# Layer 1 as eight pairs of tiles: the two tiles between the layers join the pair scheme, and the weight sums are split into parts while layer 0 still runs

## The reference

```
y0 = einsum('bct,bcd->bdt', x, W0[cond])           # layer 0, mix
x  = x + y0 @ (sign(w) * (|w| >= 0.05) * mean|w| by column) + b0
y1 = einsum('bct,bcd->bdt', x, W1[cond])           # layer 1, mix
w1 = NF4_LEVELS[q_weight] * q_scale (by groups of 64), out x in
x  = x + y1 @ w1.T + bias + 4 * (y1 @ A.T) @ B.T
```

## Time and profile before

| | |
|---|---|
| median of 3 runs | 357.35 us (357.08 to 357.49) |
| the profiled execution | 358.29 us, its span 356.5 us |
| PE busy | 348.7 us, 98% of the span |
| DVE, POOL, ACT busy | 232.8, 233.2, 165.5 us |
| chain that ended last | PE 92% |
| DMA | 44.63 MB, mean 125 GB/s |

### The profile page before, as it was taken

The page is one execution under the profiler, slowest core; times in us unless marked ns, Lnnn a source line. Parts: engine busy times, 40 slices in busy tenths (PEclk is TensorE's granted clock), DMA queues, the critical chain, the costliest instruction groups (busy, mean ns, idle before and its releaser), DMA issues.

```text
span 356.5 us, 5523 instructions
## 1 busy us (share of the span) xinstructions
PE 348.7 (98%) x1820; PEld 295.6 (83%) x1820; DVE 232.8 (65%) x354; ACT 165.5 (46%) x298; POOL 233.2 (65%) x153
## 2 busy tenths in 40 slices
PE   6899999999999999999999999999999999999996
PEld 6668788888888888888888888888888888888884
DVE  5689968999999999995859336155362552624523
ACT  2688367878887887772535305013040130411300
POOL 0388999998877987778511666567365673666632
PEclk9999999999999999999999999999999999999999
DMA  6894411753454345324421301505115042150202
GB/s 242 270 340 142 155 31 30 270 205 126 138 165 156 118 153 187 146 71 173 142 103 63 120 0 65 180 0 187 58 64 182 0 162 83 62 181 2 118 29 90
DMA packets 27838, 44.63 MB, mean 125 GB/s; under 512 B 8834, under 2 KB 17026, under 8 KB 27810
## 3 DMA queue, kind: packets, MB, share of 16 engines
q1 hardware_dynamic: 26242, 43.67, 35.3%
q10 hardware_dynamic: 1568, 0.61, 0.6%
HBM read 27.49 MB, written 16.78 MB: 124 GB/s over the span
## 4 chain that ended last, share of the span: by engine, by line
PE 92%; POOL 2%; SPq 1%; DMA 1%; ACT 1%; DVE 1%; issue 1%; POOLq 0%; ACTq 0%
PE acc L1208 37%; PE acc L1170 31%; PE xT L1134 11%; PE acc L1150 6%; PE spare L1134 4%; POOL col_scale L617 2%; PE acc L1236 2%; DMA w_in<-in_L_ffn_w 1%; PE acc L1238 1%; PE xT L1217 1%; SPq L447 0%; SPq L445 0%; SPq L466 0%; ACT w_in L718 0%; PE xT L1225 0%
## 5 line engine op out<-in xcount | busy, mean ns | idle before, releaser
L1170 PE MATMUL acc<-T,hh 128*128 128x512 f32 x192 | 76.0, 396 | 0.0
L1170 PE MATMUL acc<-T,hl 128*128 128x512 f32 x192 | 75.1, 391 | 0.0
L590 POOL TENSOR_TENSOR X<-X,bias 128x1024 f32<-128x1024 f32 x28 | 67.2, 2401 | 11.3 <-PE xT L1134 9.7
L1208 PE MATMUL acc<-W,hh 128*128 128x512 f32 x224 | 71.3, 389 | 0.0
L744 ACT ACTIVATE spare<-q_raw 128x512 f32<-128x512 int32 x96 | 56.0, 599 | 18.6 <-DVE side_p L944 6.3
L1032 DVE TENSOR_TENSOR X<-X,acc 128x512 f32<-128x512 f32 x42 | 28.8, 687 | 40.5 <-PE acc L1208 21.4
L649 POOL TENSOR_TENSOR X<-X,ys 128x512 f32<-128x512 f32 x21 | 26.4, 1286 | 36.6 <-DVE ys L1021 36.6
L1208 PEld LDWEIGHTS acc<-W,hh 128*128 128x128 f32 x224 | 42.1, 188 | 8.7
L1208 PE MATMUL acc<-W,hl 128*128 128x512 f32 x112 | 43.6, 389 | 0.0
L1170 PEld LDWEIGHTS acc<-T,hl 128*128 128x128 f32 x192 | 36.1, 188 | 7.4
L1134 PEld LDWEIGHTS xT<-mix,X 128*128 128x128 f32 x336 | 40.8, 192 | 1.4
(11 more groups left out here) (99 smaller groups left out, 652.1 us busy)
## 6 DMA issues: line engine op xcount, KB each, us to landing
out<-X SPq DMA_DIRECT2D x26, 512.0 KB, 2.9
X<-out SPq DMA_DIRECT2D x16, 512.0 KB, 3.5
X<-in_x SPq DMA_DIRECT2D x12, 512.0 KB, 3.4
q_raw<-in_L_ffn_q_weight SPq DMA_DIRECT2D x16, 256.0 KB, 2.9
w_in<-in_L_ffn_w SPq DMA_DIRECT2D x14, 256.0 KB, 6.6
x_first<-in_x SPq DMA_DIRECT2D x4, 512.0 KB, 4.2
out<-x_first SPq DMA_DIRECT2D x4, 512.0 KB, 4.7
out<-X SPq DMA_DIRECT2D x4, 256.0 KB, 2.0
```

The costliest lines, as they stand in the source:

```text
L590: pool.tensor_tensor(x_of(g), x_of(g), bias[:, :], ALU.add).then_inc(s_xb, 1)
L1170: mm = pe.matmul(acc[:, bank_of(q), :], a[:, k, :], b, start=(k == 0 and j == 0), stop=(k == KB - 1 and j == len(terms) - 1))
L1208: mm = pe.matmul(acc[:, bank, :], a[:, k, :], w1(part, c, k), start=(k == 0 and j == 0), stop=(k == HB - 1 and j == len(terms) - 1))
```

## The change

Layer 1 begins with the first pair at once: tiles 16 and 17 are pair 0 of eight (`SB` = 16). The direct multiplication, its residual add and its store are gone. B12, which only the direct tiles used, gets no high and low part; the sums are formed from the whole copy of it. The transposes of the pieces with d % 4 other than 1 come one slot earlier, so that no slot behind 30 has one.

The parts of the sums move. `SPLIT` now lists T1, T2 and T3 for the first three blocks, then their last blocks, then T4. In slot 29 (the second half of tile 14) ACT and DVE make parts 0 to 3, in slot 30 parts 4 to 8, in slot 31 part 9, behind it 10 and 11, and the four of T4 one ahead of each of the first takes of pair 0 (`LATE`), since they lie where layer 0's weight was. In slot 31 ACT also does the copy of A21 and the high part of S1, ahead of part 9; DVE does S1 to S4 ahead of it. The result of tile 15 goes into POOL's list between the low parts of S1 and S2. The first two products change places (A11 x B11, then A12 x B21), and with them the copy of the product that ACT makes. Bank 2 is free for product 2 when tile 15's second half has left it (`s_ys`), bank 3 when all sums are made. On SP tile 15's spill, then the load of tile 19, come ahead of the first pair's store.

```diff
-    SB = NT + 2
-    NP = (2 * NT - SB) // 2
+    SB = NT
+    NP = NT // 2
...
-    PRODUCTS = ((A12, B21, 0), (A11, B11, 1), (S1, T1, 2), (S2, T2, 3), (S3, T3, 0), (S4, B22, 1),
+    PRODUCTS = ((A11, B11, 0), (A12, B21, 1), (S1, T1, 2), (S2, T2, 3), (S3, T3, 0), (S4, B22, 1),
                 (A22, T4, 2))
...
-    W_ORDER = [(B11, 1), (B12, 1), (B21, 1), (B22, 1), (B11, 0), (B12, 0), (B21, 0), (B22, 0),
-               (T1, 0), (T1, 1), (T2, 0), (T2, 1), (T3, 0), (T3, 1)]
-
-
-    SPLIT = (T4, T1, T3, T2)
-    NTS = len(SPLIT)
-    SUMS_BY = (0, 4, 8, 12, NTS * HB)
+
+    W_ORDER = [(B11, 1), (B21, 1), (B22, 1), (T1, 1), (B11, 0), (B21, 0), (B22, 0), (T1, 0),
+               (T2, 0), (T2, 1), (T3, 0), (T3, 1)]
+    NW = len(W_ORDER) + 2
+
+
+    SPLIT = ([(c, j) for c in (T1, T2, T3) for j in range(HB - 1)] + [(c, HB - 1) for c in (T1, T2, T3)]
+             + [(T4, j) for j in range(HB)])
+    NTS = 4
+    SPLIT_BY = {NH * NT - 3: 0, NH * NT - 2: 4, NH * NT - 1: 9, NH * NT: 10}
+    LATE = (12, 13, 14, 15, 16)
...
-    def sums_by(m):
-
-        return SUMS_BY[m - NH * NT]
...
     def turned_in(d):
-
-        return max(NH * F, ready_in(d) + 2) + (d % 4 != 1)
+        return max(NH * F, ready_in(d) + 2)
+
+    def blocks_before(d):
+
+        return sum(BLOCK[e % 4] != B12 for e in range(d))
...
+        side_S1 = sb("side_S1", [P, 2, BANK], F32R)
+        plain_sums = sb("plain_sums", [P, KB - 2, BANK], F32)
         W_T4 = sb("W_T4", [P, 2, HB, BANK], F32R)
-        side_S1 = sb("side_S1", [P, 2, BANK], F32R)
-        plain_sums = sb("plain_sums", [P, NH * KB - 2 * HB - 2, BANK], F32)
...
-                at = w1(part, B12, {S4: 0, A22: 2}[o])
+                at = (W01 if o == S4 else W23)[:, NW - 2, part, :]
...
         def bank_free(eng, q):
             left = had_bank(q)
-            if left >= NH * NT:
-                eng.wait_ge(s_res1, left - NH * NT + 1)
-            elif left >= 0:
-                eng.wait_ge(s_ys, left + 1)
+            need(eng, s_ys, left + 1)
...
-            for g in range(NT, SB):
-                load_mix(g + 3)
-                if g == NT:
-                    spill(NT - 1)
-                else:
-                    store_one(g - 1)
-                load_x(g + 3)
             load_mix(SB + 3)
             for p in range(NP):
                 if p == 0:
-                    store_one(SB - 1)
+                    spill(NT - 1)
                     load_x(SB + 3)
...
             for g in range(F, SB):
                 if g == F:
                     result_half(F + 3)
-                elif g <= NT:
+                else:
                     result(g - 1)
                 if g > F:
                     weights_of(NH * g)
                 add_bias(g + 1)
                 weights_of(NH * g + 1)
             low_side(0, 1)
+            result(NT - 1)
             low_side(0, 2)
             add_bias(SB + 1)
             low_side(0, 3)
@@ -759,23 +750,21 @@
...
-            def high_sum(u):
-
-                j, i = divmod(u, NTS)
-                c = SPLIT[i]
-                act.wait_ge(s_made, NTS * HB)
-                if u == 0:
-                    act.wait_ge(s_acc, NH * NT)
-                if c == T2:
-                    act.wait_ge(s_Tl, NTS * j + SPLIT.index(T4) + 1)
-                act.activation(w1(0, c, j), as_is(c, j), ACT.Copy).then_inc(s_Th, 1)
+            def high_sums(start, stop):
+
+                for u in range(start, stop):
+                    c, j = SPLIT[u]
+                    act.wait_ge(s_made, NTS * j + (4 if c == T4 else 3))
+                    if u == SPLIT.index((T4, 0)):
+                        act.wait_ge(s_acc, NH * NT)
+                    act.activation(w1(0, c, j), as_is(c, j), ACT.Copy).then_inc(s_Th, 1)
...
                 if p == 0:
-                    act.wait_ge(s_acc, NH * SB if o == A22 else NH * (SB - 1))
+                    act.wait_ge(s_acc, NH * (SB - 1))
...
-                    act.wait_ge(s_acc, NH * NT)
+                    act.wait_ge(s_acc, NH * NT - 1)
...
-                act.wait_ge(s_prod, NPR * p + 2)
+                act.wait_ge(s_prod, NPR * p + 1)
...
-                act.activation(sum_of(2), acc[:, PRODUCTS[1][2], :], ACT.Copy).then_inc(s_p1, 1)
+                act.activation(sum_of(2), acc[:, PRODUCTS[0][2], :], ACT.Copy).then_inc(s_p1, 1)
...
                         if turned_in(d) == m - 1:
                             if d % 4 < 2:
                                 keep_block(d)
-                            high_w(d)
+                            if BLOCK[d % 4] != B12:
+                                high_w(d)
...
-                    if g < NT:
-                        lines(lines_by(m), lines_by(m + 1))
-                    else:
-                        for u in range(sums_by(m), sums_by(m + 1)):
-                            high_sum(u)
+                    lines(lines_by(m), lines_by(m + 1))
+                    if m + 1 in SPLIT_BY and m in SPLIT_BY:
+                        if m == NH * NT - 1:
+                            copy_A21(0)
+                            high_S(0, 1)
+                        high_sums(SPLIT_BY[m], SPLIT_BY[m + 1])
                     if m == NH * F - 2:
                         high_x(F, 0)
                         high_x(F, 1)
-            left_S(0)
+            for i in range(2, 5):
+                high_S(0, i)
+            high_sums(SPLIT_BY[NH * NT], LATE[0])
+            high_A(0, A22, 1)
             for p in range(NP):
                 copy_product(p)
+                if p == 0:
+                    high_sums(LATE[0], LATE[-1])
                 if p + 1 < NP:
...
-                if q >= NH * NT:
-                    g = q // NH
-                    dve.wait_ge(s_xb, g + 1)
-                    dve.tensor_tensor(half(g, n), half(g, n), acc[:, bank_of(q), :], ALU.add
-                                      ).then_inc(s_res1, 1)
-                    return
...
                 j, r = divmod(d, 4)
                 if r == 1:
-                    dve.wait_ge(s_asis, 2 * j + 1)
+                    dve.wait_ge(s_asis, 2 * j + 2)
                     dve.tensor_tensor(as_is(T1, j), wT_flat, as_is(T2, j), ALU.subtract).then_inc(s_made, 1)
                 elif r == 2:
-                    dve.wait_ge(s_asis, 2 * j + 2)
...
-            def low_sum(u):
-
-                j, i = divmod(u, NTS)
-                c = SPLIT[i]
-                dve.wait_ge(s_Th, u + 1)
-                dve.tensor_tensor(w1(1, c, j), as_is(c, j), w1(0, c, j).bitcast(F32), ALU.subtract
-                                  ).then_inc(s_Tl, 1)
+            def low_sums(start, stop):
+
+                for u in range(start, stop):
+                    c, j = SPLIT[u]
+                    dve.wait_ge(s_Th, u + 1)
+                    dve.tensor_tensor(w1(1, c, j), as_is(c, j), w1(0, c, j).bitcast(F32), ALU.subtract
+                                      ).then_inc(s_Tl, 1)
...
-                if i == 1:
+                if i == 0:
                     dve.wait_ge(s_p1, p + 1)
...
                         if turned_in(d) == m - 1:
-                            low_w(d)
+                            if BLOCK[d % 4] != B12:
+                                low_w(d)
                             sums_with(d)
...
-                    if g < NT:
-                        maxima(share(per, m), share(per, m + 1))
-                    else:
-                        for u in range(sums_by(m), sums_by(m + 1)):
-                            low_sum(u)
+                    maxima(share(per, m), share(per, m + 1))
                     if m == NH * SB - 1:
                         for i in range(1, 5):
                             sum_S(0, i)
+                    if m + 1 in SPLIT_BY and m in SPLIT_BY:
+                        low_sums(SPLIT_BY[m], SPLIT_BY[m + 1])
...
             leave_y(NH * SB - 1)
+            low_sums(SPLIT_BY[NH * NT], LATE[0])
             low_A(0, A22, 1)
             for p in range(NP):
                 for a in range(NTK):
+                    if p == 0 and a + 1 < len(LATE):
+                        low_sums(LATE[a], LATE[a + 1])
                     take(p, a)
...
                 for k in range(KB):
-                    if g < NT:
-                        terms = [(high(g), T0[:, n, k, :]), (low(g), T0[:, n, k, :])]
-                    else:
-                        if g == NT:
-                            pe.wait_ge(s_Wl, PIECES.index((k, n)) + 1)
-                        c = ((B11, B12), (B21, B22))[k // HB][n]
-                        wh, wl = w1(0, c, k % HB), w1(1, c, k % HB)
-                        terms = [(high(g), wh), (low(g), wh), (high(g), wl)]
-                    for j, (a, b) in enumerate(terms):
-                        mm = pe.matmul(acc[:, bank_of(q), :], a[:, k, :], b,
-                                       start=(k == 0 and j == 0),
-                                       stop=(k == KB - 1 and j == len(terms) - 1))
```

(35 more changed lines are left out.)

## The result

The changed kernel takes 359.45 us in the median of 6 runs (358.94 to 360.02), the kernel before 357.42 us in 6 (357.08 to 357.73). The ratio is 1.0056, 95% interval 1.0043 to 1.0069, so it is slower by 1.5 to 2.5 us. The profiled execution took 359.44 us.

A forecast was written before the change was run, and what follows sets the result against it. PE was taken as the bound, so the number of matmuls counts as long as nobody makes PE wait. -2.75 us for twelve fewer matmuls plus 4.7 of stalls gave +1.95, so 359.3 us, range 355.9 to 360.3.

The forecast's parts named there:

- The gain: Direct tiles 16 and 17 become a pair: twelve 512-column matmuls less on PE, -2.75 us.
- The low sums: Slots 29 and 30: DVE's low-part subtractions and POOL's instructions exclude each other and alternate; the term that decides.
- The walk: Step-by-step timing of slots 29 to 31 and the first pair with DVE and POOL alternating; chance 0.50, 357.8 to 360.3 us.
- The chain behind them: From leave_y(29) through S1 to S4 and POOL's list: product 3 starts at 183.95, product 4 at 188.6.
- The stalls: PE waits adding up to 4.7 us: 0.4 before piece 15's transpose, 0.2, 2.1 and 2.0 before products.
- The 0.4 before the last transposes: Slot 30: PE's last transpose wants T2 at 166.9, DVE has it at 167.2; a stall of 0.4 us.
- the 0.2 before product 2: First pair: PE waits for bank 2 and T1 before product 2, 0.2 us.
- +1.95: Whole kernel: -2.75 for fewer matmuls plus 4.7 us of stalls, giving 359.3 us.
- (1): Slots 29 to 31: DVE keeps the port over runs of subtractions; stall of 2.1, 356.7 us; chance 0.25.
- (2): No stall: without contention low S3 comes 0.9 us before product 4; 354.6 us; chance 0.15.
- (3): Layer 0: earlier transposes stall PE, four pieces at 0.3 each, 1.2 us on top; chance 0.10 including the unknown.
- The other parts costed at 0: Copy of A11 x B11 behind product 0, SP's spill and load order, mixing of tile 17: 0 us each.

The follow-up runs named there:

- The kernel with both edits: Changed kernel with POOL's low S2 ahead of result 15, low S3 ahead of bias add 17, and two POOL waits for low sums: 354.52 us, ratio 0.9924.
- the kernel after: The changed kernel itself, against the kernel before: 359.45 us, ratio 1.0056.

## Why the prediction was right

**The gain.** -2.75 us for twelve matmuls holds. The kernel with both edits has all the parts of the change and lies 2.79 us below the kernel before (2.2 to 3.2), and its first pair takes 22.64 us. From the start of the steady work to the last take it is 328.57 - 325.85 = 2.72 us shorter, the prediction's twelve times 0.227. By the 131 ns that the prediction quotes from the Trainium skill, "TensorE: Matmul & The Clock Gate", section on the back-to-back issue gap, it would have been 1.6; the trace doesn't agree.

**The low sums.** The walk had slot 29's four ending 5.8 us behind T1 (measured 5.6) and slot 30's five taking 5.0 (4.94). That a held subtraction ends some 0.55 us behind POOL's instruction, and that the two alternate, was right: POOL's scale and bias add of 158.79 and 160.14 lie inside DVE's run of four, and are held themselves, to 1.38 and 2.81 us.

**The chain behind them.** leave_y(29) 164.7 (measured 164.0), S1 made at 175.7 (175.0), low S1 to 177.8 (177.0), leave_y(31) to 178.95 (178.1), result 15 to 182.0 (181.2), product 3 at 183.95 (183.0), low S3 to 188.5 (187.4), product 4 at 188.6 (187.5). All are 0.7 to 1.1 early, 0.45 of it because this execution's steady work began earlier by that. The stalls were put at 4.7 us. Measured are 3.88 in the pair and 0.39 before it, 4.3. The 0.4 before the last transposes came as forecast; the 0.2 before product 2 didn't come. Product 3 came 1.9 late and not 2.1, product 4 another 1.8 and not 2.0, with 0.25 more behind it until its matmuls ran as usual (12 in 2.97 us). Order and places of the gaps were as predicted, and what ended the last two was POOL's low parts, though the profile names something else (the last section has this).

**The sum.** +1.95 was forecast, +2.03 measured (1.5 to 2.5). The count of PE's own time gives -2.75 + 4.27 = +1.52, and the two profiles differ by 1.51 from the start of the steady work on. The half microsecond between that and the medians is open; the start of the steady work varies by more than that between executions (23.6 to 24.8 us), and one profile of each kernel can't tell whether it varies by kernel. So the forecast sum is right in its mechanism, but that it came within 0.1 us is luck: the stalls were put 0.4 us too high, and the medians show 0.5 more than the stalls explain.

**The rivals.** (1), DVE keeping the port, is refuted by POOL's instructions inside its runs. (2), no stall, is refuted for this kernel. Its time is what the kernel with both edits reaches, 354.6 us against 354.5 measured, but not its way: low sums and adds are still held there (four low sums in 3.48 us), only PE no longer waits for what comes late. (3) has one place where the earlier transposes cost by themselves, some 0.2 us, and only while B12's low part is still made; in the changed kernel they cost the 0.4 us before the last piece, which the walk had as its own term. The other parts costed at 0 show nothing: all of the loss is in the three gaps and came back when these closed.

## What to carry to other kernels

An instruction with two operands in SBUF on DVE and one that reads SBUF on POOL acted as one resource here, however idle each engine looked. Place DVE's runs of such work where POOL has something to wait for anyway, or make POOL wait; that cost two semaphore waits here and gave 2.5 us. Look for durations above the usual one of the same shape, since a held instruction counts as busy (5.64 us for four low sums, with no idle time ahead of them). And in a list that works strictly in order, put what PE waits for ahead of adds that nobody waits for yet: that alone gave 3.6 us.

## What the runs showed of the hardware

The exclusion has a size and an order. A held subtraction of 512 columns ends 0.55 us behind the POOL instruction that held it (so for every held low sum of the traces that have them), and costs POOL's next instruction 0.3 to 0.5 us (scaling 1.38 against 1.05, adds of 1024 columns 2.81 to 2.90 against 2.4, low part 1.71 to 1.75 against 1.3). The two engines take turns even when both have their instructions queued back to back. A memset of 256 columns on DVE kept its 0.27 us beside every add and held none up. A DVE sum with one input in PSUM kept its 0.68. But two inputs in SBUF are not the only case: the cast of 34.30 in the earlier trace rows, the second of two, has a single input, in SBUF, and was held for 1.29 us by POOL's add of 34.25.

The chain of the kernel after names a DVE add as product 4's releaser:

```profile
186.17 0.68 DVE X L1021
...
187.47 2.97 PE acc L1193 x12
```

It ended at 186.85. The POOL instruction that ended at 187.37, 0.10 us before the product began, is the low part of S3. Where it was moved ahead of the bias add, together with low S2 ahead of the result, the gap of 1.50 us shrank to 0.46. A releaser in the chain is an inference from times, and the program has to be read beside it.
